# Low-rank A, B and three small pieces of work moved in the opening and the adapter stage of a two-layer kernel

## The chip, the cores and the metric

One of the eight cores of a Trainium2 chip runs the kernel. The time is device microseconds of one launch; the median of 3 runs of the kernel before is 611.19 us (611.18 to 611.63). Everything is float32; TensorE work that is written as float32r is split by hand into a leading part and a rest.

## The reference

`x` is 32 sequences of 64 tokens of 1024 features, with one adapter id (0 to 15) per sequence. Cut to what matters:

```python
c   = einsum('bsi,boi->bso', x, weight[ids])            # a 1024x1024 adapter per sequence
h   = c @ lora_A.T ; logits = c @ W_router.T            # rank 16, 8 experts
w   = normalised top-2 of softmax(logits)
x   = x + c @ W_base.T + b_base + 2 * einsum(h, lora_B, w)
x   = x + ffn(weights1[ids] applied to x)               # 16 heads of 64, hidden 256, exact gelu, features permuted
```

## The kernel before, in words

**Stage 1, the adapters.** The sequences are sorted by id on the chip and worked as 16 pairs, t = 0 to 15. A pair is 8 blocks (k = 0 to 7) of 8 matmuls on TensorE (PE); block k of pair t needs x of the pair (`x_in`, two halves in turn, fetched on ScalarE's DMA queue by `load_x`, L876) and the k-th 128 rows of one or two adapters (`ring`, 512 KB each, on SyncE's (SP's) queue, `load_pair`, L332). The rows of pair t + 1 are asked for when block k of pair t is done (`block_done`), those of pair 1 at once behind the eight of pair 0. Pair 0 has both its sequences on one adapter (`twin_blocks`, L551); the others go through `adapter_blocks` (L535). Between blocks 4 and 5 of pair t, PE does `router(t - 1)` (L571): low-rank A and the router weights, `ar_sb`, 1024 rows of 136 floats (544 bytes) in HBM, against pair t - 1's transposed result `c_pair`. PE waits for `ar_in`, the landing of `ar_sb`, at L622, after pair 0 and ahead of the first block of pair 1.

**VectorE (DVE)** takes each pair's result out by `turn_pair(t)` (L1102, 16 transposes of 32x256 straight from PSUM), then does one more piece of work, then `route(t)` (L1121: a copy at L1135, top-2 and the weights, a chain of 16 small instructions that ends in `hw_four`). In a loop of three rounds (i) over four pairs (n = 0 to 3, t = 4i + 1 + n), that one more piece is a third of a 128x1024 tile of W_base for n < 3 (`turn_tile`, L1182), and for n = 3 `turn_four` (L1197), which transposes four pairs' `hw_four` into `hw_lines` by 16 transposes of 32x128. ScalarE (ACT) then copies `hw_lines` out (`hw_put`, L901). `turn_four` waits for four routes and for the copies of the round before.

**GpSimd (POOL)** moves each `c_pair` into `c_all` (`keep_pair`, L461), then issues gathers by row index: rows of W_base (`raw_tile`) after pairs 0, 4 and 8, and for t in `GATHERS` (L63, pairs 4 to 11) one 128-row piece of low-rank B and of the bias (L479 to L482). B is read by PE at the end of stage 1 (L639), the bias by DVE behind L1242.

**The opening.** SP, ACT and POOL start DMAs at once: ACT the ids and then `ar_sb` (L848), POOL five gathers of W_base of 512 KB (L459), which PE transposes (`turn_base`, L589) and ACT copies back (`base_copied`, L888) before pair 0 starts. ACT's first use of its function table is that copy. DVE sorts in the meantime and releases x and the first adapter by `lists_ok`. `stay_busy` (L596) is eight idle transposes of PE between W_base and pair 0.

**The end of stage 1.** DVE does `turn_pair(14)`, three subtractions (`base_rest`, L1177), two register loads of sequence numbers (`last_seqs`, L249), and `hw_turned`, `route(14)`. Stage 2 (L1245 on) is then 32 steps bound by PE and is not touched.

Of the kernel before, what the change touches and what calls it, by code (L numbers as in the profile page):

```python
# [35 lines left out]
P = 128  # L36
# [6 lines left out]
KT = D // P  # L43
SQ = 32
PAIRS = SEQS // 2
# [14 lines left out]
BUSY = 8  # L60
BATCHED = PAIRS - 4
TILE_PIECES = (range(0, 6), range(6, 11), range(11, 16))
GATHERS = range(PAIRS // 4, PAIRS // 4 + KT)  # L63


def build(nc, xT, x_seq, ids, adapters, w_base, b_base, lora_a_router, lora_b, mix, up, down, perm, out):
# [3 lines left out]
    with ctx:  # L70
        def sem(name):
            return ctx.enter_context(nc.semaphore(name))
# [10 lines left out]
        def at(offset, name, shape, dt=F32):  # L83
# [62 lines left out]
        ar_sb = at(ar_at, "ar_sb", [P, KT, AR])  # L146
# [21 lines left out]
        ident = at(region(0.5), "ident", [P, P])  # L168
# [8 lines left out]
        m1, m2, gap, th, best1, best2, w1, w2 = (  # L177
            (small[5] if i < 4 else small[6])[:, 2 * (i % 4):2 * (i % 4) + 1] for i in range(8))
# [14 lines left out]
        def base_set(j):  # L193
# [11 lines left out]
        ids_in, sort_ids_in, perm_in, ar_in, b_in, bias_in, mix_in, up_in = (  # L205
            sem(n) for n in ("ids_in", "sort_ids_in", "perm_in", "ar_in", "b_in", "bias_in", "mix_in", "up_in"))
# [9 lines left out]
        ident_ok, consts, number_ok, sorting, placed_ok, sorted_done, order_ok = (  # L216
            sem(n) for n in ("ident_ok", "consts", "number_ok", "sorting", "placed_ok", "sorted_done", "order_ok"))
        base_four_ok = sem("base_four_ok")
        loads_ok, lists_ok, tile_in, tile_turned, hw_turned_ok, hw_placed = (
            sem(n) for n in ("loads_ok", "lists_ok", "tile_in", "tile_turned", "hw_turned_ok", "hw_placed"))  # L220
# [5 lines left out]
        router_done, gap_ok, tanh_ok, chain, hw_ok, hw_tr_done, hw_t_ok = (  # L226
            sem(n) for n in ("router_done", "gap_ok", "tanh_ok", "chain", "hw_ok", "hw_tr_done", "hw_t_ok"))
# [21 lines left out]
        def last_seqs(eng):  # L249

            return [eng.value_load(order[0:1, 2, (z + 1) * PAIRS - 1:(z + 1) * PAIRS], min_val=0, max_val=SEQS - 1)
                    for z in range(2)]
# [171 lines left out]
        def _(pool):  # L424
# [47 lines left out]
            for t in range(PAIRS - 1):  # L472
                keep_pair(t)
                if t % 4 == 0 and t // 4 < KT - SOON:
                    j = t // 4 + SOON
                    if t > 0:
                        pool.wait_ge(tile_turned, t // 4)
                    gather(raw_tile[:, :], w_base, perm_sb[:, j:j + 1], tile_in)
                if t in GATHERS:  # L479
                    j = t - GATHERS[0]  # L480
                    gather(b_rows[:, j, :], lora_b, perm_sb[:, j:j + 1], b_in)
                    gather(bias[:, j:j + 1], bias_rows, perm_sb[:, j:j + 1], bias_in)  # L482
            pool.wait_ge(base_hi_ok, 5)
# [361 lines left out]
        def _(act):  # L845
            act.dma_start(all_ids[:, :], ids.rearrange("(a s) -> a s", a=1).broadcast_to([SEQS, SEQS])) \
                .then_inc(sort_ids_in, 16)
            act.dma_start(ar_sb[:, :, :], lora_a_router.rearrange("(k p) e -> p k e", p=P)).then_inc(ar_in, 16)  # L848


            def out_of_acc(t, half):
# [24 lines left out]
            def load_x(t, half):  # L876

                for z in range(2):
                    seq = act.value_load(order[0:1, 2, bass.ds(t + z * PAIRS, 1)], min_val=0, max_val=SEQS - 1)
                    act.dma_start(x_in[:, half, z, :, :],  # L880
                                  x_seq[bass.ds(seq, 1), :, :, :].rearrange("a p k t -> p (a k) t")) \
                        .then_inc(x_in_in[half], 16)
# [25 lines left out]
                            .then_inc(hw_placed, 1)  # L908

            act.sem_inc(hw_placed, 8)  # L910
            act.wait_ge(lists_ok, 1)
            load_x(0, 0)
            for j in range(SOON):
                base_copied(j)
            load_x(1, 1)
            for half in range(2):
                next_x(half, half)
                tanh(half)
# [12 lines left out]
            seqs = last_seqs(act)  # L931
# [101 lines left out]
        def _(dve):  # L1033
# [68 lines left out]
            def turn_pair(t, half):  # L1102

                dve.wait_ge(block_done, (t + 1) * KT)
                dve.wait_ge(c_kept, t * 2 + 2)
                for q in range(P // SQ):
                    for r in range(P // SQ):
                        last = nc.vector.transpose(  # L1108
                            c_pair[r * SQ:(r + 1) * SQ, :, q * SQ:(q + 1) * SQ],
                            wide[half][q * SQ:(q + 1) * SQ, :, :]  # L1110
                            .rearrange("p h (k r f) -> p (h k) r f", k=KT // 2, f=SQ)[:, :, r, :])
                last.then_inc(c_pair_ok, 2)
# [8 lines left out]
            def route(t, hw_out=hw[:, :]):  # L1121

                n = [0]

                def link(ins):

                    n[0] += 1
                    ins.then_inc(chain, 1)  # L1130
                    dve.wait_ge(chain, t * LINKS + n[0])

                logits = h_l[:, ER:AR]
                dve.wait_ge(router_done, t + 1)
                link(nc.vector.tensor_copy(h_l[:, :], router_ps[:, 0:AR]))  # L1135
                link(nc.vector.reduce_max(m1, logits, AX_X))
                link(nc.vector.scalar_tensor_tensor(out=score[:, :], in0=logits, scalar=m1,
                                                    in1=ahead[:, :], op0=ALU.is_equal, op1=ALU.mult))
                link(nc.vector.reduce_max(best1, score[:, :], AX_X))
                link(nc.vector.tensor_scalar(first[:, :], score[:, :], best1, None, ALU.is_equal))  # L1140
                link(nc.vector.scalar_tensor_tensor(out=rest[:, :], in0=first[:, :], scalar=BIG,
                                                    in1=logits, op0=ALU.mult, op1=ALU.add))
                link(nc.vector.reduce_max(m2, rest[:, :], AX_X))
                nc.vector.tensor_tensor(gap, m1, m2, ALU.subtract).then_inc(gap_ok, 1)  # L1144
                link(nc.vector.scalar_tensor_tensor(out=score[:, :], in0=rest[:, :], scalar=m2,
                                                    in1=ahead[:, :], op0=ALU.is_equal, op1=ALU.mult))
                link(nc.vector.reduce_max(best2, score[:, :], AX_X))
                link(nc.vector.tensor_scalar(second[:, :], score[:, :], best2, None, ALU.is_equal))
                dve.wait_ge(tanh_ok, t + 1)
                nc.vector.tensor_scalar(w1, th, 1.0, None, ALU.add)  # L1150
                link(nc.vector.tensor_scalar(w2, th, -1.0, 1.0, ALU.mult, ALU.add))
                link(nc.vector.tensor_scalar(mixw[:, :], first[:, :], w1, None, ALU.mult))
                link(nc.vector.scalar_tensor_tensor(out=mixw[:, :], in0=second[:, :], scalar=w2,
                                                    in1=mixw[:, :], op0=ALU.mult, op1=ALU.add))
                nc.vector.tensor_tensor(hw_out.rearrange("p (e r) -> p e r", r=RANK),
                                        h_l[:, 0:ER].rearrange("p (e r) -> p e r", r=RANK),
                                        mixw[:, :].rearrange("p (e a) -> p e a", a=1).broadcast_to([P, EXPERTS, RANK]),
                                        ALU.mult).then_inc(hw_ok, 1)
                assert n[0] == LINKS
# [34 lines left out]
                if pieces[-1] == 15:  # L1194
                    last.then_inc(tile_turned, 1)

            def turn_four(i):  # L1197


                dve.wait_ge(hw_ok, i * 4 + 4)  # L1200
                dve.wait_ge(hw_placed, i * 8 + 8)
                for q in range(P // SQ):
                    for r in range(P // SQ):
                        last = nc.vector.transpose(hw_lines[q * SQ:(q + 1) * SQ, :, r * SQ:(r + 1) * SQ],
                                                   hw_four[r * SQ:(r + 1) * SQ, :, q * SQ:(q + 1) * SQ])
                last.then_inc(hw_turned_ok, 1)

            def pair(t, half):
                turn_pair(t, half)
                hw_turned(t - 1)  # L1210
                route(t)
# [3 lines left out]
            with dve.Fori(0, KT - SOON) as i:  # L1215
                for n in range(4):
                    t = i * 4 + 1 + n
                    turn_pair(t, (n + 1) % 2)
                    if n < 3:
                        turn_tile(i, TILE_PIECES[n])  # L1220
                    else:
                        turn_four(i)
                    route(t, hw_four[:, (n + 1) % 4, :])
            pair(PAIRS - 3, 1)
            turn_pair(PAIRS - 2, 0)
            for j in SPLIT_ORDER[0:3]:
                base_rest(j)
            seqs = last_seqs(dve)
            hw_turned(PAIRS - 3)
            route(PAIRS - 2)  # L1230
            out_of_acc(PAIRS - 1, 1)
# [164 lines left out]
```

## Time and profile before

| | us |
|---|---|
| median of 3 runs | 611.19 |
| time of the profiled execution | 612.55 |
| span of its profile | 610.7 |
| PE busy, of the span | 593.5 (97%) |
| DVE busy | 471.6 (77%) |
| ACT, POOL busy | 144.7, 128.5 |
| mean DMA traffic | 175 GB/s |

The span is that of the profiled execution, from its first instruction to its last; 1.85 us of that execution's own time lie around it. Times in the rows count from the span's start. Stage 1 ends near 276 us.

### The profile page before, as it was taken

Reading aid. Unit: us, or ns where it says so; the run is one execution under the profiler, and the core shown is the slowest. Engines: PE = TensorE matmul, PEld = TensorE weight load, DVE = VectorE, ACT = ScalarE, POOL = GpSimd, SP = SyncE. Lnnn points to the kernel's source line nnn. Section 1 sums busy time; section 2 is a strip of 40 time slices with the busy share of each in tenths; the row PEclk is TensorE's granted clock in tenths of the full one; section 3 lists DMA queues with packets and bytes.
Section 4 is the critical chain, followed back from the end, with each engine's and each line's share of the span. In section 5 each row is a group of like instructions: output and inputs, shape, how many; then the busy total and the mean of one; then the engine's idle time right before and its main releaser. Section 6 shows DMA issues by size and latency. Waiting matters only on the chain.

```text
span 610.7 us, 13500 instructions
## 1 busy us (share of the span) xinstructions
PE 593.5 (97%) x4383; PEld 349.0 (57%) x4384; DVE 471.6 (77%) x1303; ACT 144.7 (24%) x290; POOL 128.5 (21%) x195
## 2 busy tenths in 40 slices
PE   4999999999998999989999999999999999999997
PEld 3344444344433444457767676767676767676773
DVE  3068778878887779698888897879987889887863
ACT  3100000200020002154333523225342325231324
POOL 4010002121111220060022231313131313131312
PEclk9999999999999999999999999999999999999999
DMA  8998998998999987111022222222232223231322
GB/s 264 407 394 315 309 301 293 325 312 301 315 409 402 355 310 254 44 59 39 17 65 90 74 87 71 87 71 91 63 94 68 88 64 97 62 93 60 94 72 86
DMA packets 43427, 106.90 MB, mean 175 GB/s; under 512 B 8450, under 2 KB 17666, under 8 KB 43394
## 3 DMA queue, kind: packets, MB, share of 16 engines
q1 hardware_dynamic: 30914, 76.04, 36.0%
q0 software_dynamic: 6784, 21.51, 10.6%
q10 hardware_dynamic: 5696, 8.95, 4.3%
q8 instruction: 16, 0.26, 0.2%
q14 instruction: 17, 0.14, 0.1%
HBM read 98.09 MB, written 8.39 MB: 174 GB/s over the span
## 4 chain that ended last, share of the span: by engine, by line
PE 86%; DVE 6%; DMA 4%; issue 1%; DVEq 0%; SPq 0%; ACTq 0%; POOL 0%; another core or an unknown queue 0%
PE wide L546 26%; PE bank L653 20%; PE bank L661 10%; PE bank L741 8%; PE wide L724 8%; PE y_wide L577 4%; DVE c_pair L1108 3%; DMA ring<-adapters_dram 3%; PE y_wide L699 3%; PE wide L561 2%; DMA x_in<-x_seq_dram 1%; PE bank L674 1%; PE bank L677 1%; PE bank L673 1%; PE bank L754 1%
## 5 line engine op out<-in xcount | busy, mean ns | idle before, releaser
L546 PE MATMUL wide<-ring,x_in 128*64 128x512 f32 x960 | 209.5, 592 | 1.8 <-DMA ring<-adapters_dram 1.5
L546 PEld LDWEIGHTS wide<-ring,x_in 128*64 128x64 f32 x960 | 73.0, 137 | 126.7 <-issue 126.7
L1306 DVE STREAM_TRANSPOSE x_tok<-xres 32x128 f32<-32x128 f32 x464 | 140.3, 302 | 6.0
L1108 DVE STREAM_TRANSPOSE c_pair<-wide 32x256 f32<-32x256 f32 x240 | 107.1, 446 | 39.5 <-issue 22.1
L955 ACT ACTIVATE act_sb<-wide 128x512 f32<-128x512 f32 x120 | 66.3, 608 | 191.3 <-PE wide L724 191.3
L653 PE MATMUL bank<-c_hi,base_t 128*128 128x512 f32 x384 | 102.3, 390 | 0.0
L430 POOL DMA_INDIRECT xres<-xT_dram,row_in x32 | 34.3, 1073 | 230.1 <-DVE out_sb L1296 226.8
L653 PEld LDWEIGHTS bank<-c_hi,base_t 128*128 128x128 f32 x384 | 71.9, 188 | 15.4
L661 PE MATMUL bank<-c_lo,base_t 128*128 (+1 forms) x256 | 78.0, 390 | 0.0
L468 POOL COPY c_all<-c_pair 128x512 f32 x30 | 19.4, 672 | 213.7 <-DVE c_pair L1108 213.7
L870 ACT ACTIVATE small<-small 128x1 f32<-128x1 f32 x16 | 3.2, 203 | 218.2 <-DVE small L1144 218.2
L741 PE MATMUL bank<-act_sb,down_sb 64*64 64x512 f32 x224 | 54.3, 602 | 0.0
L741 PE MATMUL wide<-act_sb,down_sb 64*64 64x512 f32 x224 | 54.3, 602 | 0.0
L661 PEld LDWEIGHTS bank<-c_lo,base_t 128*128 128x128 f32 x256 | 48.1, 188 | 10.3
L1287 DVE TENSOR_TENSOR xres<-wide,xres 128x512 f32<-128x512 f32 x28 | 19.4, 692 | 27.1 <-PE wide L741 27.1
L1260 DVE SCALAR_TENSOR_TENSOR xres<-bank,bias,xres 128x512 f32<-128x512 f32 x32 | 23.9, 749 | 19.4 <-PE bank L677 19.4
L653 PE MATMUL bank<-c_hi_slots,base_t 128*128 (+1 forms) x128 | 38.1, 419 | 0.0
L577 PEld LDWEIGHTS y_wide<-ar_sb,c_pair 128*64 128x64 f32 x512 | 30.4, 137 | 9.4 <-issue 6.1
L577 PE MATMUL y_wide<-ar_sb,c_pair 128*64 128x136 f32 x512 | 32.7, 280 | 1.2 <-DVE c_pair L1117 0.8
L495 POOL DMA_INDIRECT out_dram<-out_sb,row_out x28 | 28.5, 1017 | 8.5 <-issue 8.5
L653 PEld LDWEIGHTS bank<-c_hi_slots,base_t 128*128 128x128 f32 x128 | 21.6, 188 | 13.8 <-issue 10.9
L699 PEld LDWEIGHTS y_wide<-mix_now,x_tok 64*64 64x64 f32 x960 | 19.5, 134 | 16.2 <-issue 16.2
(166 smaller groups left out, 605.1 us busy)
## 6 DMA issues: line engine op xcount, KB each, us to landing
ring<-adapters_dram SPq DMA_DIRECT2D x128, 512.0 KB, 5.9
x_in<-x_seq_dram ACTq DMA_DIRECT2D x32, 256.0 KB, 4.9
down_sb<-down_dram SPq DMA_DIRECT2D x32, 128.0 KB
up_raw<-up_dram SPq DMA_DIRECT2D x62, 64.0 KB
ar_sb<-lora_a_router_dram ACTq DMA_DIRECT2D x1, 544.0 KB, 4.3
mix_sb<-mix_dram SPq DMA_DIRECT2D x32, 16.0 KB
xres<-xT_dram,row_in POOLq DMA_INDIRECT x32, 3.4
out_dram<-out_sb,row_out POOLq DMA_INDIRECT x28, 2.9
```

The lines of the kernel that those rows point to most:

```text
L430: pool.indirect_dma_start(dst, None, table, bass.IndirectOffsetOnAxis(ap=rows, axis=0)) \
L495: pool.indirect_dma_start(out_rows, bass.IndirectOffsetOnAxis(ap=row_out[:, j:j + 1], axis=0), src, None).then_inc(stored, 16)
L546: last = pe.matmul(acc[half][h][z * TOK:(z + 1) * TOK, :], x_in[:, half, z, k, :], ring[:, k, z, h * HALF:(h + 1) * HALF], start=(k == 0), ...
L577: last = pe.matmul(router_ps[toks, 0:AR], c_pair[:, k, toks], ar_sb[:, k, :], start=(k == 0), stop=(k == KT - 1), skip_group_check=True)
L653: pe.matmul(c_bank(g, j)[:, :], base_t[:, j, w, k, :], c_hi_row(g, k), start=(k == 0 and w == 0), stop=False)
L661: last = pe.matmul(c_bank(g, j)[:, :], base_t[:, j, 0, k, :], c_lo[:, k, bass.ds(g * GT, GT)], start=False, stop=False)
L699: last = pe.matmul(y_wide[h * HD:(h + 1) * HD, z, p * TOK:(p + 1) * TOK], x1_tok[rows, p * P + h * HD:p * P + (h + 1) * HD], mix_now[rows, ...
L724: last = pe.matmul(u_ps[2 * m + head][:, :], w[rows, m * P:(m + 1) * P], y[rows, :], start=(n == 0), stop=(n == 2))
L741: last = pe.matmul(ps[head * HD:(head + 1) * HD, :], down_sb[rows, j % 2, head, m, :], act_sb[rows, 2 * m + head, :], start=(m == 0), stop ...
L955: nc.scalar.activation(act_of(g, j)[:, i, :], u_ps[i][:, :], ACT.Gelu).then_inc(act_ok, 1)
L1108: last = nc.vector.transpose(c_pair[r * SQ:(r + 1) * SQ, :, q * SQ:(q + 1) * SQ], wide[half][q * SQ:(q + 1) * SQ, :, :] .rearrange("p h (k ...
L1306: last = nc.vector.transpose(x1_tok[q * SQ:(q + 1) * SQ, :].rearrange("p (c f) -> p c f", f=P)[:, :, f * SQ:(f + 1) * SQ], xres[f * SQ:(f ...
```

## The change

It consists of five pieces. The load of `ar_sb` moves from ACT's second instruction to behind `load_x(1, 1)`, the load of x of pair 1; PE's wait at L622 stays. The pieces of B and bias are gathered after pairs 1 to 8 (0-based; the second to the ninth) and no longer after 4 to 11. `turn_four` is cut in two: a quarter of it (4 transposes) goes behind `route` of n = 2, the other three quarters stay at n = 3. ACT makes a one-column copy of `ident` before it waits for the sorted lists, so that its table is loaded there. DVE's `last_seqs` moves ahead of `turn_pair(14)`.

```diff
-GATHERS = range(PAIRS // 4, PAIRS // 4 + KT)
+GATHERS = {j + 1: (j,) for j in range(KT)}
...
-                if t in GATHERS:
-                    j = t - GATHERS[0]
+                for j in GATHERS.get(t, ()):
                     gather(b_rows[:, j, :], lora_b, perm_sb[:, j:j + 1], b_in)
                     gather(bias[:, j:j + 1], bias_rows, perm_sb[:, j:j + 1], bias_in)
...
             act.dma_start(all_ids[:, :], ids.rearrange("(a s) -> a s", a=1).broadcast_to([SEQS, SEQS])) \
                 .then_inc(sort_ids_in, 16)
-            act.dma_start(ar_sb[:, :, :], lora_a_router.rearrange("(k p) e -> p k e", p=P)).then_inc(ar_in, 16)
...
             act.sem_inc(hw_placed, 8)
+            act.wait_ge(ident_ok, 2)
+            nc.scalar.copy(th, ident[:, 0:1])
             act.wait_ge(lists_ok, 1)
             load_x(0, 0)
             for j in range(SOON):
                 base_copied(j)
             load_x(1, 1)
+            act.dma_start(ar_sb[:, :, :], lora_a_router.rearrange("(k p) e -> p k e", p=P)).then_inc(ar_in, 16)
...
-            def turn_four(i):
-                dve.wait_ge(hw_ok, i * 4 + 4)
-                dve.wait_ge(hw_placed, i * 8 + 8)
-                for q in range(P // SQ):
+            def turn_four(i, qs):
+                if qs[0] == 0:
+                    dve.wait_ge(hw_ok, i * 4 + 4)
+                    dve.wait_ge(hw_placed, i * 8 + 8)
+                for q in qs:
...
-                last.then_inc(hw_turned_ok, 1)
+                if qs[-1] == P // SQ - 1:
+                    last.then_inc(hw_turned_ok, 1)
...
                     if n < 3:
                         turn_tile(i, TILE_PIECES[n])
                     else:
-                        turn_four(i)
+                        turn_four(i, range(1, 4))
                     route(t, hw_four[:, (n + 1) % 4, :])
+                    if n == 2:
+                        turn_four(i, range(0, 1))
             pair(PAIRS - 3, 1)
+            seqs = last_seqs(dve)
             turn_pair(PAIRS - 2, 0)
             for j in SPLIT_ORDER[0:3]:
                 base_rest(j)
-            seqs = last_seqs(dve)
```

## Rows read from the trace of the kernel before

**Rows 1.** The page: span, busy us by engine, issue of A (KB, us to landing).

```profile
span 610.7 us, 13500 instructions
...
PE 593.5 (97%) x4383; PEld 349.0 (57%) x4384; DVE 471.6 (77%) x1303; ACT 144.7 (24%) x290; POOL 128.5 (21%) x195
...
ar_sb<-lora_a_router_dram ACTq DMA_DIRECT2D x1, 544.0 KB, 4.3
```

**Rows 2.** Waits of PE, 0 to 300 us: sum in us, times, longest.

```profile
PE wide L546 <- DMA ring<-adapters_dram: 1.5, 2, 1.3
...
PE y_wide L577 <- DVE c_pair L1108: 0.5, 1, 0.5
```

**Rows 3.** Chain of waits, 0 to 45 us: start, us, what.

```profile
10.19 8.06 DMA x_in<-x_seq_dram
...
18.29 13.95 PE wide L561 x64
32.24 8.58 PE wide L546 x40
```

**Rows 4.** Timeline of PE, 7 to 19 us: start, us, what, [idle before <-releaser].

```profile
7.33 1.09 PE L526 MATMUL bank<-ident,base_rows 128*128 128x128 f32 x4 [2.53 <-DMA base_rows<-w_base_dram,perm_sb]
...
12.24 0.60 PE L526 MATMUL bank<-ident,base_rows 128*128 128x128 f32 x4
```

**Rows 5.** Timeline of ACT and its queue, same columns.

```profile
1.16 0.45 ACTq L848 DMA_DIRECT2D ar_sb<-lora_a_router_dram  x1
9.08 1.46 ACTq L880 DMA_DIRECT2D x_in<-x_seq_dram  x2
10.57 1.28 ACT L891 ACT_TABLE_LOAD   x1 [10.44 <-issue]
```

**Rows 6.** DMA queues, 2.2 to 5.2 us: packets, MB, share of 16 engines.

```profile
q10 hardware_dynamic: 1040, 0.56, 68.7%
q0 software_dynamic: 21, 0.09, 22.9%
```

**Rows 7.** DMA queues, 9.7 to 25.3 us.

```profile
q1 hardware_dynamic: 1059, 3.88, 62.0%
```

**Rows 8.** DMA queues, 20.6 to 25.3 us.

```profile
q1 hardware_dynamic: 380, 1.37, 73.7%
q10 hardware_dynamic: 287, 0.52, 29.5%
```

**Rows 9.** DMA queues, 25.3 to 32 us.

```profile
q1 hardware_dynamic: 744, 2.72, 101.6%
```

**Rows 10.** Source view of line 338, 16 to 24 us: durations ns min/median/max.

```profile
L338 SPq DMA_DIRECT2D ring<-adapters_dram x8: 333/340/1415, 16.9 to 22.2; - x8
```

**Rows 11.** Windows at the end: busy us of PE, PEld, DVE, ACT, POOL; granted clock; DMA.

```profile
606.00:608.00 2.00, 0.89 (x10) 0.29 (x5) 0.85 (x2) 0.00 (x0) 1.32 (x2) 1.00 0.18 63
...
609.00:610.00 1.00, 0.00 (x0) 0.00 (x0) 0.00 (x0) 0.00 (x0) 0.00 (x0) 0.72 0.68 262
```

**Rows 12.** Timeline of DVE around pairs 3 to 7, same columns as rows 4.

```profile
94.73 7.34 DVE L1108 STREAM_TRANSPOSE c_pair<-wide 32x256 f32<-32x256 f32 x16 [1.73 <-PE wide L546]
102.11 5.05 DVE L1204 STREAM_TRANSPOSE hw_lines<-hw_four 32x128 f32<-32x128 f32 x16
107.91 0.30 DVE L1135 COPY h_l<-y_wide 128x136 f32<-128x136 f32 x1 [0.76 <-remote]
...
111.82 7.34 DVE L1108 STREAM_TRANSPOSE c_pair<-wide 32x256 f32<-32x256 f32 x16 [0.40 <-issue]
...
157.76 7.34 DVE L1108 STREAM_TRANSPOSE c_pair<-wide 32x256 f32<-32x256 f32 x16 [0.37 <-PE wide L546]
```

**Rows 13.** Timeline of POOL, pair 4.

```profile
106.19 0.95 POOL L430 DMA_INDIRECT bias<-b_base_dram,perm_sb  x1 [0.31 <-issue]
```

**Rows 14.** Timeline of DVE, pair 14.

```profile
254.10 7.34 DVE L1108 STREAM_TRANSPOSE c_pair<-wide 32x256 f32<-32x256 f32 x16 [1.64 <-PE wide L546]
261.47 4.32 DVE L1179 TENSOR_TENSOR base_t<-base_rows,base_t 128x1024 fp32r<-128x1024 f32 x3
```

## The prediction

> **What bounds the kernel now.** The page first: PE is busy 593.5 of 610.7 us [rows 1], so an edit gains only where PE waits, and loses wherever it makes PE wait anew. The waits of PE over stage 1 are few: 1.5 us for adapter rows, once 1.3 us, and 0.5 us for one pair's transposes [rows 2]. The chain of the opening says what starts PE: x of pair 0, 8.06 us under way, lands at 18.25, PE begins pair 0 at 18.29 and pair 1 without a gap at 32.24 [rows 3]. All of this hangs on the DMA engines, so the queues come next. SP's queue alone fills them: from 25.3 to 32 us it takes 101.6% of 16 engines [rows 9].
>
> **A behind x of pair 1.** This is the part that decides. PE's wait for A stays ahead of pair 1, so A must be in by 32 us. What stands behind that wait is the whole adapter stream, then everything else on PE.
>
> What A costs the queue: its 1024 packets of 544 bytes took 68.7% of 16 engines for 3.0 us, over 65 packets an engine 32 ns each [rows 6]. At its old place nothing else wanted the engines: A had moved 0.56 MB by 5.2 us, the gathers of W_base 0.09 [rows 6], and A landed at 1.16 + 4.3 = 5.5 us [rows 1, 5]. The start therefore gains little: at least 0, at most the 2.1 us that A kept the engines. I take 0.2, the nearer row being that the gathers hardly met it. The table load of 1.28 us [rows 5] comes off ACT's first copy of W_base, but x is sent ahead of it, at 9.08, and x is what PE waits for: 0.
>
> At its new place A goes behind x of pair 1 in the same queue, whose packets run from 20.6 to 25.3 us [rows 8], and all the while SP's queue is full. How two queues share is seen there. x is 0.52 MB in packets of 2 KB, 16 an engine; beside it SP's queue moved 1.37 MB, 21 packets of 4 KB an engine. A share by bytes would have let x pass beside 0.52 MB. So the engines take turns by packet, and a small packet waits for a large one each time. A packet of SP's queue is 161 ns (2.72 MB, 664 packets, 41.5 an engine, in 6.7 us) [rows 9]. A is 64 packets an engine, twice 32, so 64 turns of 161 + 32 ns: 12.35 us. With x over at 25.3 - 0.2 = 25.1, A's last packet ends at 37.45, and with the 0.3 us from there to the landing as at the old place it is in at 37.8. Is SP's queue full so long? Of its first 16 loads (8.39 MB, pair 0 and half of pair 1) 3.88 MB are through by 25.3 [rows 7]; 4.51 MB are left, 69 packets an engine, over 64. That gives the upper bound as well: 25.3 + 69 x 0.161 + 64 x 0.032 + 0.3 = 38.8, and 0.7 for a slower engine (x took 4.7 us where 16 turns are 4.0 [rows 8]). Pair 1 starts at 37.8 instead of 32.24: **+5.6**, in the bounds 0 (rival 1) and +7.3.
>
> PE then idles some 5.8 us, and its clock is at stake. After PE's last work at 606.9 us the granted clock is 0.72 of full over 609 to 610 [rows 11], so it fell from 2.4 to 1.2 GHz after about 2.5 idle us. In the opening the first transposes ran 1.09 us for four, the later ones 0.60, from 12.2 us on: 4.7 us after work began [rows 4]. PE would restart at 1.2 GHz and, if it takes as long, lose half of 4.7: **+2.35**, bounds 0 and 2.35; I take the upper one since the idle time is over twice 2.5.
>
> Loads for pair 2 are asked for as pair 1's blocks end and so come later by as much, on engines that are then less full: no further loss, and none of the delay is won back, since PE sets the pace after it.
>
> **`turn_four` in two.** Sixteen transposes take 5.05 us, 0.32 each [rows 12]; four moved are 1.26 us less at pair 4. That is the pair whose lateness PE feels: `turn_pair(5)` began at 111.82, and router(5) waited 0.5 us [rows 2]. The four go behind route(3), where DVE idled 1.73 us before pair 4's transposes [rows 12]. But the gathers of B are now at pair 3 too, and they cost DVE time: at pair 4 the bias gather ended at 107.14 [rows 13], and route's first copy, ready at 107.16, began at 107.91; at pair 7, which had a gather, DVE idled only 0.37 us before the next pair's transposes, against 1.73 at pair 3 without one [rows 12]. So cover falls from 1.73 to 0.37, pair 4's transposes start about 0.9 us late, within 0.1 us of what router(4) allows: +0.05. Net of that DVE is 1.26 - 0.9 = 0.3 us earlier, plus 0.76 if its copy now comes ahead of the bias gather instead of behind it: the wait of 0.46 goes. If the copy falls behind the gather, the gain turns into 0.8 us of loss. I take **-0.4**, bounds -0.5 and +0.8. In the third round nothing is short.
>
> **B in pairs 1 to 8.** It removes 16 packets of gathered rows from pair 9, ahead of the one long wait for adapter rows (1.3 us [rows 2]); 64 KB is 16 packets of 4 KB, one an engine, 0.16 us and as much again at its edge for the bias: **-0.2**, bounds 0 and -0.3. POOL itself has time in every pair.
>
> **Register values ahead of pair 14.** DVE idles 1.64 us before pair 14's transposes, which hides them; where they stood they ran under three subtractions of 4.32 us that DVE's engine was busy with [rows 14]: 0 either way.
>
> The sum: +5.6 + 2.35 - 0.4 - 0.2 = +7.3 us (the 0.2 of the start is in the first term). Against the profiled execution, 612.55 us (span 610.7 and 1.85 around it), that is 619.9; the median is 1.36 us lower, so **618.5 us**. In this forecast's own range stand 615.5 (clock kept, A at 37) to 621.5 (all upper bounds).
>
> **Rivals.**
>
> 1. *A gets through in time.* If a turn takes many small packets, A is quick: 64 packets (2.0 us) behind eight of SP's (1.3 us) end at 28.4, in at 28.7, ahead of 32.04. It decides at 6.6 us over 64 packets, 0.10 us a packet: below it PE does not wait. Then the sum is -0.2 - 0.4 - 0.2: 610.4 us. Against it stand rows 8, where x had at most one packet for each of SP's. The Trainium skill (DMA: Bandwidth & Descriptors, Queues, rings and completion order) has this rule: an engine drains about 9 to 17 descriptors, at most 64, from one ring before it switches. With all 64 in one turn that would be this rival; with 17 for A and SP's loads of 8 an engine it would be four turns and a landing near 32.7. The trace does not decide it for packets of 544 bytes. Chance 0.16.
>
> 2. *A holds up SP's queue.* SP's loads stood up to 1415 ns at issue where 333 are usual [rows 10]: something fills up. If A's 1024 packets keep SP's last three loads back, SP's queue has 45 packets an engine beside A: 25.1 + 45 x 0.193 + 19 x 0.032 + 0.3 = 34.7, +2.5, and with the other terms +1.9: 613.1 us; 615.4 if the clock falls in that wait. Chance 0.13.
>
> 3. *The start was held by A after all.* Then up to 2.1 us come back, and if A is also in time the kernel takes 608.8 us. Against: rows 6. Chance 0.06. With the forecast's stall it would only shift it.
>
> 4. *The halved `turn_four` does not do what it should*, because the copy falls behind the bias gather: 1.2 us more, 619.7, a third of the forecast's chance and inside it.
>
> **How the numbers follow.** The forecast has 0.64, the rest 0.01. A measurement of this kernel can tell 0.2% from no change, 1.22 us: slower means over 612.4. Slower: the forecast and nearly all of rival 2, 0.76; same: rival 1 and a little of 2, 0.18; faster: rival 3, 0.06. The range leaves out rivals 1 and 3: 611.5 to 621.5, rival 2 with A still earlier as its lower end.
>
> **What would show it.** Right: PE waits for the landing of A at pair 1, about 5.8 us from 32; the queue of ACT has 1024 packets from 25 to 37 us beside a full queue of SP; pair 1's first matmuls start at twice their spacing; router(5) without its 0.46 us; pair 10's wait for adapter rows at 1.1 us; the table load near 2 us and x of pair 0 within 0.3 us of 18.2. Wrong: A's packets in one bunch between 25 and 29 us with SP's queue standing still, or a gap in SP's queue after 30 us, or pair 0 that starts a microsecond or more earlier.

## The result and the profile after

The changed kernel takes 621.51 us (median of 4 runs, 619.02 to 623.77) against 611.40 us before (4 runs, 611.18 to 611.63): the ratio is 1.0164, with a 95% interval of 1.0125 to 1.0204. The profiled execution of the changed kernel took 623.77 us, 2.3 us over its median; the profiled execution before took 612.55.

First the page of the changed kernel, the lines that answer to [rows 1]:

```profile
span 622.0 us, 13501 instructions
...
PE 597.7 (96%) x4383; PEld 356.6 (57%) x4384; DVE 471.6 (76%) x1303; ACT 145.2 (23%) x291; POOL 128.5 (21%) x195
...
ar_sb<-lora_a_router_dram ACTq DMA_DIRECT2D x1, 544.0 KB, 19.3
```

The span is 11.3 us longer and PE is only 4.2 us busier, on the same 4383 matmuls. So most of the loss is PE standing still, and a part is matmuls that take longer. A needs 19.3 us from issue to landing where it needed 4.3.

The waits of PE from 0 to 300 us, which answer to [rows 2] (sum in us, times, longest):

```profile
PE wide L545 <- issue: 7.7, 1, 7.7
...
PE wide L525 <- DMA base_rows<-w_base_dram,perm_sb: 3.1, 2, 2.8
...
PE wide L545 <- DMA ring<-adapters_dram: 1.1, 2, 0.6
PE bank L584 <- DVE hw_four L1156: 1.0, 1, 1.0
```

One wait is new, 7.7 us at L545. Router(5)'s 0.5 us is gone, and 1.1 us of waits for adapter rows are left of 1.5. The wait of 1.0 us for `hw_four` of pair 14 is as before. The new wait is put down to "issue", which names nothing. The chain of waits says what is in it (start, us, what; it answers to [rows 3]):

```profile
8.01 9.27 DMA base_rows<-w_base_dram,perm_sb
...
17.32 1.98 PE wide L525 x8
...
21.43 19.30 DMA ar_sb<-lora_a_router_dram
40.73 1.75 issue
42.49 11.50 PE wide L545 x40
53.99 1.85 PE y_wide L576 x32
```

A lands at 40.73, and only then come 1.75 us of something else, before pair 1's first block. The timeline of PE gives the rest (start, us, what, [idle before <-releaser]):

```profile
17.32 1.97 PE L525 MATMUL wide<-ident,base_rows 128*128 128x128 f32 x8 [2.80 <-DMA base_rows<-w_base_dram,perm_sb]
...
20.82 13.95 PE L560 MATMUL wide<-ring,x_in 128*64 128x512 f32 x64
42.49 11.50 PE L545 MATMUL wide<-ring,x_in 128*64 128x512 f32 x40 [7.71 <-issue]
...
198.29 1.94 PE L545 MATMUL wide<-ring,x_in 128*64 128x512 f32 x8 [0.45 <-DMA ring<-adapters_dram]
200.83 10.52 PE L545 MATMUL wide<-ring,x_in 128*64 128x512 f32 x48 [0.60 <-DMA ring<-adapters_dram]
```

From this the 11.3 us of this execution can be added up (40 matmuls at 8.75 us are in the timelines of experiments 1 and 3):

- The opening is 2.53 us longer: pair 0 starts at 20.82 instead of 18.29 [rows 3]. PE waits 2.80 us for the fifth gathered tile of W_base, then transposes it slowly (eight in 1.97 us). Below it turns out that this belongs to this execution, not to the change.
- PE waits for A from the end of pair 0 (20.82 + 13.95 = 34.77) to 40.73: 5.96 us.
- The 1.75 us behind the landing.
- Pair 1's first 40 matmuls take 11.50 us; the same 40 take 8.75 where PE has not stood still: 2.75 us.
- Together 12.99. Back come 0.46 us at router(5), and 0.78 at the adapter rows (0.45 + 0.60 here; before 0.23 + 0.32 + 1.28). The 0.45 us that are left are small gaps not assigned to anything.

The clock stands in the windows (from:to and length in us; busy time and count of PE, PEld, DVE, ACT, POOL; granted clock, share of the DMA engines, GB/s):

```profile
34.80:37.70 2.90, 0.00 (x0) 0.00 (x0) 2.73 (x7) 0.00 (x0) 0.00 (x0) 1.00 1.03 389
37.70:40.70 3.00, 0.00 (x0) 0.00 (x0) 2.92 (x7) 0.00 (x0) 0.00 (x0) 0.50 0.71 258
42.50:48.00 5.50, 5.50 (x14) 1.90 (x16) 0.00 (x0) 0.00 (x0) 2.13 (x3) 0.50 0.41 107
48.00:54.00 6.00, 6.00 (x32) 2.23 (x30) 0.00 (x0) 0.00 (x0) 0.00 (x0) 1.00 0.76 249
```

PE stops at 34.8. Some 3 us later the granted clock drops to 0.50, which is 1.2 GHz. It stays there through the wait and for 5.5 us of work after it: 14 matmuls in 5.5 us, then 32 in 6.0.

Last the DMA queues from 29 to 37 us, which answer to [rows 9] (packets, MB, share of 16 engines):

```profile
q1 hardware_dynamic: 752, 2.73, 86.6%
q10 hardware_dynamic: 750, 0.41, 17.3%
```

SP's queue (q1) moved 752 packets of 4 KB while ACT's queue (q10) moved 750 of 544 bytes: one for one. Over the same 8 us the kernel before moved 825 and 133. A's 1024 packets ran from 27.45 to 40.12 us, 12.7 us; alone they took some 3 [rows 6].

### The profile page after: what moved, and what is told of

It is laid out like the page before. It is cut to its first block, busy times and chain, and to the rows that moved or that the text cites. A ratio compares the mean times of both kernels' runs of the same rounds, so it can differ in the third digit from the quotient of the medians.

```text
span 622.0 us, 13501 instructions
## 1 busy us (share of the span) xinstructions
PE 597.7 (96%) x4383; PEld 356.6 (57%) x4384; DVE 471.6 (76%) x1303; ACT 145.2 (23%) x291; POOL 128.5 (21%) x195
## 4 chain that ended last, share of the span: by engine, by line
PE 87%; DMA 7%; DVE 2%; issue 1%; POOL 1%; ACTq 0%; DVEq 0%; SPq 0%; ACT 0%
PE wide L545 29%; PE bank L652 20%; PE bank L660 9%; PE bank L740 8%; PE wide L723 8%; PE y_wide L576 4%; DMA ar_sb<-lora_a_router_dram 3%; PE y_wide L698 2%; DMA ring<-adapters_dram 2%; DMA base_rows<-w_base_dram,perm_sb 1%; PE bank L672 1%; PE bank L676 1%; PE bank L673 1%; DVE c_pair L1109 1%; PE bank L753 1%
## 5 line engine op out<-in xcount | busy, mean ns | idle before, releaser
L545 PE MATMUL wide<-ring,x_in 128*64 128x512 f32 x960 | 212.2, 598 | 8.8 <-issue 7.7
L545 PEld LDWEIGHTS wide<-ring,x_in 128*64 128x64 f32 x960 | 77.7, 138 | 131.7 <-issue 131.7
L1265 DVE SCALAR_TENSOR_TENSOR xres<-bank,bias,xres 128x512 f32<-128x512 f32 x32 | 23.9, 749 | 19.4 <-PE bank L676 19.4
L576 PE MATMUL y_wide<-ar_sb,c_pair 128*64 128x136 f32 x512 | 32.7, 279 | 0.8 <-DVE c_pair L1118 0.8
## 6 DMA issues: line engine op xcount, KB each, us to landing
ar_sb<-lora_a_router_dram ACTq DMA_DIRECT2D x1, 544.0 KB, 19.3
```

The costliest lines, as they stand in the source:

```text
L545: last = pe.matmul(acc[half][h][z * TOK:(z + 1) * TOK, :], x_in[:, half, z, k, :], ring[:, k, z, h * HALF:(h + 1) * HALF], start=(k == 0), ...
L576: last = pe.matmul(router_ps[toks, 0:AR], c_pair[:, k, toks], ar_sb[:, k, :], start=(k == 0), stop=(k == KT - 1), skip_group_check=True)
```

## The experiments

Eleven runs, on chips that also ran the kernel before. Where a kernel was timed in several rounds, the 95% interval of the ratio stands with it. The expectations of experiments 1 to 4 counted on 1.9 us that the changed kernel seemed to win back between pairs 5 and 10. No time shows them: experiments 1, 3 and 4 came out 1.4, 1.4 and 1.8 us above what was expected, experiment 2 came out 1.7 us below.

**1. A back at the front, the rest of the change kept** (a_front).

```diff
+            act.dma_start(ar_sb[:, :, :], lora_a_router.rearrange("(k p) e -> p k e", p=P)).then_inc(ar_in, 16)
...
             load_x(1, 1)
-            act.dma_start(ar_sb[:, :, :], lora_a_router.rearrange("(k p) e -> p k e", p=P)).then_inc(ar_in, 16)
```

> The changed kernel with the load of low-rank A back at ACT's second instruction; the other four pieces stay. Theory (all of the loss is A's new place): A lands near 5.5 us, no wait ahead of pair 1, pair 0 begins near 18.3 us, and the 1.9 us that the changed kernel won back between pairs 5 and 10 stay: 609.5 us. Rival one (the early table load or something else moved the opening): pair 0 begins near 20.8 us, 611 to 612 us. Rival two (the small pieces gain nothing by themselves, PE only waited less because it came later): 611.2 us.

Measured: 610.86 us (10 runs) against 611.34 (25 runs), ratio 0.9986 (0.9966 to 1.0005). A lands 4.3 us after its issue. The timeline of PE:

```profile
17.77 13.95 PE L560 MATMUL wide<-ring,x_in 128*64 128x512 f32 x64 [1.85 <-DMA x_in<-x_seq_dram]
31.55 8.75 PE L545 MATMUL wide<-ring,x_in 128*64 128x512 f32 x40
```

Pair 1 follows pair 0 without a gap and at full speed. Everything in the change except A's place is worth a gain of at most 0.34% by this interval, or nothing; experiment 9 narrows it.

**2. Only A moved, the rest as before** (a_only): in the kernel before, the same one line moved.

```diff
-            act.dma_start(ar_sb[:, :, :], lora_a_router.rearrange("(k p) e -> p k e", p=P)).then_inc(ar_in, 16)
...
             load_x(1, 1)
+            act.dma_start(ar_sb[:, :, :], lora_a_router.rearrange("(k p) e -> p k e", p=P)).then_inc(ar_in, 16)
```

> The kernel before with nothing but A's load moved behind x of pair 1. Theory: the same wait of some 7.7 us ahead of pair 1, half clock after it, and without the gains at pairs 5 and 10: 1.9 us more than the changed kernel, near 623.4 us. Rival (another piece has a part in the stall): at or under the changed kernel's 621.5 us.

Measured: 621.72 us (4 runs) against 611.34, ratio 1.0158 (1.0123 to 1.0193). The chain:

```profile
19.37 19.42 DMA ar_sb<-lora_a_router_dram
38.79 1.75 issue
40.55 10.86 PE wide L546 x40
```

The one line makes the whole loss, with the same three pieces: pair 0 ends at 18.52 + 13.95 = 32.47 and A lands at 38.79 (6.32 us), 1.75 us follow, and 40 matmuls take 10.86. Here pair 0 began at 18.52, so the late opening of the changed kernel's profile does not come with A. Nor was there a wait at router(5), though B's gathers were late in this kernel and its `turn_four` whole.

**3. PE's wait for A moved behind the blocks that don't read A** (wait_late).

```diff
-            pe.wait_ge(ar_in, 16)
             landed = landings(1)
             adapter_blocks(0, 1, range(0, 3), landed)
             adapter_blocks(0, 1, range(3, 5), landed)
+            pe.wait_ge(ar_in, 16)
             router(0)
```

> The changed kernel with PE's wait for A moved from ahead of pair 1 to ahead of router(0), five blocks later; A's load itself is as late as in the changed kernel. Theory (only the wait's place makes A's slow arrival cost anything): A again takes about 19 us from issue to landing, but router(0) wants it near 43 us, so PE does not wait, the clock stays at full rate; 609.5 us if pair 0 begins at 18.3 us, 612 us if it begins at 20.8 us. Rival (the adapter stream is held up by A's packets): PE waits for adapter rows in pair 1 instead, 613 us or more.

Measured: 610.91 us (10 runs) against 611.34, ratio 0.999 (0.9974 to 1.0005). The view of the tile `ar_sb`, then the timeline of PE:

```profile
L916 ACTq DMA_DIRECT2D ar_sb<-lora_a_router_dram x1: 457/457/457, 19.6 to 19.6; - x1
...
DMA to landing us min/median/max: 19.2/19.2/19.2
```

```profile
32.45 8.75 PE L545 MATMUL wide<-ring,x_in 128*64 128x512 f32 x40
41.03 2.02 PE L576 MATMUL y_wide<-ar_sb,c_pair 128*64 128x136 f32 x32
```

A is as late as in the changed kernel (19.6 + 19.2 = 38.8), and nothing waits for it: pair 1 starts at once, and router(0), the first reader, at 41.03. So the slow load alone costs nothing, and it doesn't hold up adapter rows. What costs is a wait placed 8.6 us ahead of the first reader. The margin is about 2 us.

**4. A in 128 packets of 4352 bytes** (a_wide). The same numbers lie in DRAM in another order, so that each partition reads one run; the wait stays where the change has it.

```diff
-            act.dma_start(ar_sb[:, :, :], lora_a_router.rearrange("(k p) e -> p k e", p=P)).then_inc(ar_in, 16)
+            act.dma_start(ar_sb[:, :, :], lora_a_router.rearrange("p (k e) -> p k e", e=AR)).then_inc(ar_in, 16)
...
+        .reshape(KT, P, AR).transpose(1, 0, 2).reshape(P, KT * AR),
```

> The changed kernel with A laid out in HBM as one contiguous run of 4352 bytes per partition, 128 pieces instead of 1024, at the same late place and with the same wait of PE. Theory (the engines take turns by packet, so the count of packets sets A's time beside a full queue): 8 packets an engine, 8 turns of 161 + 170 ns or 2.7 us; A lands 3 to 4 us behind x of pair 1, near 30 us, no wait at pair 1; 609.5 us (612 us with the late opening). Rival (its place behind x or its bytes make A late): it lands near 40 us as before and the time is 619 to 622 us.

Measured: 611.32 us (10 runs) against 611.34, ratio 0.9995 (0.9979 to 1.001). A lands 10.8 us after its issue at 18.0, ahead of the end of pair 0 at 31.8. The queues from 23.9 to 28 us, in which A passed:

```profile
q1 hardware_dynamic: 296, 1.09, 66.1%
q10 hardware_dynamic: 162, 0.57, 35.4%
```

The same bytes in an eighth of the packets pass in 4 us instead of 12.7. So it is mainly the number of packets, not of bytes, that fixes how long this load takes beside a full queue. The count isn't one for one here: SP's queue moved 296 packets beside 162, of which 128 are A's.

**5. A in 512 packets of 1088 bytes** (a_half), for a second point on that line.

```diff
-            act.dma_start(ar_sb[:, :, :], lora_a_router.rearrange("(k p) e -> p k e", p=P)).then_inc(ar_in, 16)
+            act.dma_start(ar_sb[:, :, :].rearrange("p (k z) e -> p k (z e)", z=2), lora_a_router.rearrange("(k p) e -> p k e", p=P)).then_inc(ar_in, 16)
...
+        .reshape(KT // 2, 2, P, AR).transpose(0, 2, 1, 3).reshape(KT // 2 * P, 2 * AR),
```

> The changed kernel with A in 512 packets of 1088 bytes instead of 1024 of 544. Theory (turns by packet): 32 turns of 161 + 48 ns, 6.7 us where 1024 packets took 12.3 to 12.8 and 128 took some 3; A's time from issue to landing falls from 19.3 to about 13.5 us, PE waits about 2 us and the register loads behind it, mostly at full clock: 612 to 615 us. Rival (packets of less than 2 KB are slow by themselves whatever their count, or the effect is all or nothing): landing as for 544 bytes and 621 us, or as for 4352 bytes and 611.3 us.

Measured: 615.32 us (7 runs, 612.85 to 618.65) against 611.76 (10 runs), ratio 1.0059 (1.0025 to 1.0093). The queues from 26 to 33 us, then the chain:

```profile
q1 hardware_dynamic: 617, 2.24, 80.3%
q10 hardware_dynamic: 520, 0.55, 22.4%
```

```profile
19.83 14.36 DMA ar_sb<-lora_a_router_dram
34.20 1.85 issue
36.05 8.80 PE wide L545 x40
```

A's packets took 7.8 us, from 25.8 to 33.6. With 8, 32 and 64 packets an engine (experiment 4, this one, the changed kernel) they took 4.1, 7.8 and 12.7 us: 0.155 us for each further packet an engine in the first step, 0.153 in the second, on top of some 2.8 us, at the same number of bytes. That is about one packet of SP's queue (0.161 us, worked out in the prediction from [rows 9]) for each of A's. The short end varies, though: in experiment 10 the same 128 packets took 3.1 us, and by that point the first step is 0.19 us a packet.

PE stood still for 2.02 us here, nearly all of it the piece behind the landing, and the clock held: 40 matmuls in 8.80 us. But the wait for A itself was only 0.17 us, since pair 0 began late, at 19.28, and took 14.75 us instead of 13.95: after 3.05 us of idle time in the opening the granted clock was at 0.50 from 17.5 to 20.9. So about half of this execution's loss is its opening and not A. The time came out 0.3 us over the range expected, and the runs lie apart: three took 612.85 to 613.45 us at a mean granted clock of 0.999 to 1.0, three 616.4 to 618.65 at 0.991 to 0.994, which is what the changed kernel's runs have (0.989 to 0.994). That PE lost its clock at the wait for A in these three is likely, but none of them was profiled.

**6. The register loads ahead of the wait** (loads_first). What stands between A's wait and pair 1's first block is `landings(1)` (L531), two loads of a register from SBUF. In the kernel before nothing held PE's sequencer there, so they ran ahead while PE worked.

```diff
-            pe.wait_ge(ar_in, 16)
             landed = landings(1)
+            pe.wait_ge(ar_in, 16)
```

> The changed kernel with PE's four-instruction register load (landings) for pair 1 ahead of the wait for A instead of behind it. In the changed kernel's chain 1.75 us lie between A's landing at 40.73 us and pair 1's first matmul at 42.49. Theory (these are the register loads, which ran under pair 0 as long as A was early): the gap falls below 0.3 us and the time by 1.5 us, to 620.0 us. Rival (the 1.75 us are something that every long wait of PE costs on waking): the gap and the time, 621.5 us, stay.

Measured: 619.71 us (4 runs) against 611.76, ratio 1.0129 (1.0106 to 1.0153), 1.8 us under the changed kernel's median. The chain:

```profile
38.84 0.04 issue
38.89 10.69 PE wide L545 x40
```

The 1.75 us are gone: 0.04 us from landing to first matmul. They were the register loads, which a wait ahead of them had turned from hidden to exposed. The gap shows this; the times alone would not, since one run of the changed kernel took 619.02 us as well.

**7. PE kept busy in the wait** (kept_warm): 64 transposes into a bank that holds nothing then, ahead of the wait. They add work whose result is not used.

```diff
+            for _ in range(64):
+                pe.transpose(bank7[:, 0:P], ident[:, :], ident[:, :])
             pe.wait_ge(ar_in, 16)
```

> The changed kernel with 64 idle transposes of PE (some 7 us at full rate) into an unused bank between pair 0 and the wait for A; the wait ends when it did. Theory (pair 1 lost 2.7 us to the half clock that PE's idling brought): the granted clock stays at full rate, the five blocks ahead of router(0) take 8.7 us instead of 11.5, and the time is 2.1 to 2.7 us less than the changed kernel's 621.5: 619 us. Rival (pair 1's first blocks are slow because the adapter rows or x are late): 621.5 us or more.

Measured: 620.78 us (4 runs, 619.29 to 621.61) against 611.76, ratio 1.0155 (1.0129 to 1.018); the profiled execution took 619.29. The timeline of PE, then the window of pair 1's first blocks:

```profile
31.92 7.21 PE L622 MATMUL bank<-ident 128*128 128x128 f32 x64
40.57 1.94 PE L545 MATMUL wide<-ring,x_in 128*64 128x512 f32 x8 [1.44 <-issue]
```

```profile
40.60:49.20 8.60, 8.60 (x41) 3.47 (x43) 0.00 (x0) 0.00 (x0) 1.24 (x2) 1.00 0.71 243
```

The profile settles it: with PE at work the granted clock stays at 1.00, and the 40 matmuls take 8.80 us in the chain. The mean granted clock of the four runs is 0.997 to 1.0, against 0.989 to 0.994 in the changed kernel. The times don't settle it: the median is 0.7 us under the changed kernel's and not the 2.1 to 2.7 expected, within the spread of four runs of either. A part of the difference is in the profile. A landed at 38.9 (19.08 + 19.8), 6.9 us after pair 0's end at 31.99, the last idle transpose ended at 39.13, and pair 1 began at 40.57. That is 8.58 us from pair to pair where the changed kernel's first profile has 7.71 and its second 6.51, so some of what the clock gave back went into a longer stall. The slow clock is shown as a cost of 1.9 to 2.75 us in the profiles, and not measured as a difference of times.

**8. The kernel before, profiled a second time** (before_again), since two terms of the prediction rested on delays seen once.

> The kernel before, unchanged, for a second profile. Open is whether the two delays in the first one are the kernel's own: route's first copy 1.4 us late at pairs 6, 7, 10 and 11 and 0.8 us late at pairs 4 and 8, and with it router(5)'s wait of 0.46 us. If they come from the gathers of low-rank B they stand at the same pairs again; if they belong to that one execution they are gone or elsewhere, as in the kernel with A alone moved, which kept those gathers and showed none.

Measured: 611.93 us, span 610.1. The timeline of DVE at pair 4, against [rows 12], then the waits of PE from 0 to 300 us:

```profile
102.06 5.05 DVE L1204 STREAM_TRANSPOSE hw_lines<-hw_four 32x128 f32<-32x128 f32 x16
107.15 0.30 DVE L1135 COPY h_l<-y_wide 128x136 f32<-128x136 f32 x1
```

```profile
PE wide L546 <- DMA ring<-adapters_dram: 2.2, 3, 1.0
```

The route copy follows the transposes at once; the 0.76 us ahead of it in the first profile and router(5)'s wait are not there. Both belonged to one execution.

**9. A at the front, timed longer** (a_front_5): the kernel of experiment 1.

> The changed kernel with A's load back at the front once more, over more rounds, for what the other four pieces are worth: the profiles so far show PE waiting 1.2 to 1.6 us for adapter rows after pair 8 with low-rank B gathered early against 1.5 to 2.2 us with it late. Theory (B's gathers took that from the adapter rows): 0.3 to 0.6 us below the kernel before, ratio 0.9990 to 0.9995. Rival (the pieces also free the opening): ratio 0.998 or less. Second rival (nothing): 1.000.

Measured: 611.19 us (11 runs, 610.71 to 612.26) against 611.25 (21 runs), ratio 1.0002 (0.9992 to 1.0011). The rest of the change has no effect within 0.11%.

**10. The wide layout and the late wait together** (both): the edits of experiments 3 and 4, as the version most likely to beat both kernels.

> The changed kernel with A in 128 packets and PE's wait for it ahead of router(0), still behind x of pair 1: the late place without any of its costs. Theory (A's old place did not delay the opening, since the W_base gathers hardly meet it): the same as with A at the front, 610.9 us, and pair 0 begins between 17.7 and 19.3 us as elsewhere. Rival (moving A away frees the opening, hidden so far by the packets of 544 bytes): pair 0 begins near 17 us and the time is 609.5 us.

Measured: 610.93 us (11 runs) against 611.25, ratio 0.9993 (0.998 to 1.0007). A lands 9.9 us after its issue and nothing waits. It repairs the loss, and any gain over the kernel before is at most 0.2%.

**11. The changed kernel, profiled a second time** (after_again).

> The changed kernel unchanged, for a second profile of the opening. In the first one the fifth gather of W_base landed at 17.3 us, PE idled 2.8 us for it, did its transposes at half clock and began pair 0 at 20.8 us; elsewhere it began between 17.8 and 19.3. If the late gather belongs to the one execution, pair 0 begins before 19.5 us here and the time is 1 to 3 us less than that execution's 623.8; if A's absence from the front makes it late each time, it is 20 us or more again. A's 1024 packets again take 12 to 13 us and PE idles 7.5 to 8.2 us.

Measured: 619.2 us, span 617.4. The chain:

```profile
16.95 19.00 DMA ar_sb<-lora_a_router_dram
35.95 1.76 issue
37.71 11.36 PE wide L545 x40
```

Pair 0 began at 17.25 here and at 20.82 in the first profile, and that is most of the 4.6 us between the two executions. A was issued 4.5 us sooner than in the first profile and pair 0 began only 3.6 sooner, so the wait for A was shorter: 35.95 - 17.25 - 13.95 = 4.75 us. PE idled 6.5 us in all, under the 7.5 to 8.2 expected. A's packets ran from 22.9 to 35.3 us, 12.4 us, as expected. What moved the wait is when A was issued: 0.3 us ahead of pair 0's start here, 0.6 behind it in the first profile.

## Why the prediction was right in kind and short in size

The forecast was 618.5 us, in a range to 621.5; the measured median lies at that upper end. Four profiles hold the stall: the changed kernel twice, A alone, and the loads ahead of the wait. Their means say what each term was worth.

- **The wait for A**, forecast +5.6. Measured 5.96, 6.32, 6.43 and 4.75: mean 5.87. The step that led there, turns by single packets, held: 752 against 750 packets in 8 us, and 64 turns took 12.7 us where 12.35 were forecast. Experiments 4 and 5 show it as cause: fewer packets, same bytes, shorter load.
- **The rule of the Trainium skill** (DMA: Bandwidth & Descriptors, Queues, rings and completion order), by which an engine drains some 9 to 17 descriptors of one ring ahead of the next, puts the landing, as estimated in the prediction, near 32.7, some 0.7 us behind the 32.04 at which rival 1 has no wait. Here 752 packets of one queue went beside 750 of the other, and A landed at 38.8 (experiment 2): the trace disagrees, and the measurement decides.
- **The half clock**, forecast +2.35. Measured 2.75, 2.11, 1.94 and 2.61 (40 matmuls against 8.75 us): mean 2.35. That the mean falls on the forecast is in part luck: in the same order the granted clock fell 3.0, 5.4, 3.4 and 4.9 us after PE's last work, not 2.5, and came back 5.5, 4.2, 3.8 and 5.2 us after it began again, where the prediction had 4.7 (its own row gives 12.24 - 7.33 = 4.9). PE idle for 6.4 to 8.1 us brought the clock down each time; idle for 2.02 us (experiment 5) and 2.34 us (the opening of experiment 3) did not, while idle for 2.80 us (the opening of the changed kernel) and 3.05 us (that of experiment 5) was followed by a granted clock of 0.50. Keeping PE at work kept it up (experiment 7).
- **What was missing: +1.75.** This is the step that failed. The prediction says "What stands behind that wait is the whole adapter stream, then everything else on PE"; it did not list the sequencer's own instructions, `landings(1)`, the register loads that the blocks' waits need. Rows of before show them nowhere, since they ran ahead under PE's work. Experiment 6 takes them from behind the wait: the gap falls from 1.75 to 0.04 us, and the median by 1.8.
- **`turn_four` in two**, forecast -0.4. It does what it says, as DVE's timeline of the changed kernel shows:

```profile
106.29 1.24 DVE L1206 STREAM_TRANSPOSE hw_lines<-hw_four 32x128 f32<-32x128 f32 x4
107.89 7.34 DVE L1109 STREAM_TRANSPOSE c_pair<-wide 32x256 f32<-32x256 f32 x16 [0.35 <-PE wide L545]
115.26 3.79 DVE L1206 STREAM_TRANSPOSE hw_lines<-hw_four 32x128 f32<-32x128 f32 x12
119.08 0.30 DVE L1136 COPY h_l<-y_wide 128x136 f32<-128x136 f32 x1
```

  Four of 16 stand a pair earlier, in 1.24 us, and the copy comes 1.26 us sooner after the pair's transposes. But the wait it was to remove was not there in experiment 8, nor in experiment 2 with `turn_four` whole. The term was read from one execution's accident; where that delay is absent its size is 0. The account of B's gathers costing DVE 0.9 us falls with it: with B early (experiments 1 and 4) the copy starts within 0.03 us of the transposes' end. Rival 4 falls as well.
- **B earlier**, forecast -0.2. Waits for adapter rows after pair 8 sum to 1.4 and 1.5 us (A at the front), 1.2 (experiments 3, 4 and 7), 1.6 (experiments 5 and 6), 1.8 (experiment 10) and 1.05 and 1.4 (the changed kernel) with B early; 1.8 and 2.2 before, 1.65 in experiment 2 with B late. That leans to a gain of some 0.4 us, though the two groups overlap. The times of experiments 1, 3, 4, 9 and 10, 0.02 to 0.48 us under the kernel before with intervals that all hold 1, can't confirm it.
- **The opening**, forecast -0.2 within the first term, bound -2.1. Pair 0 began at 18.29 and 18.25 before, and between 17.25 and 20.82 in the changed kernel; with A at the front at 17.77 and 18.33, with A late in experiments 2 to 7 and 10 at 17.86 to 19.28. No place of A orders these. What varies is when the fifth gathered tile of W_base lands (its transposes begin between 13.70 and 17.32) and, behind it, x of pair 0: in 10 of the 13 profiles PE's last wait ahead of pair 0 is for x, 0.2 to 1.9 us. A gain of 2.1 us from the opening (rival 3) is in none of the times, and the spread between executions here, over 3 us, is larger than the term.
- **The table load** was costed at 0 and moved as expected; so were the **register values** ahead of pair 14: PE's wait for that pair's `hw_four` is 1.0 us in both kernels. The timeline of ACT:

```profile
1.24 1.28 ACT L910 ACT_TABLE_LOAD   x1 [1.11 <-PEq L1394]
...
21.43 0.46 ACTq L916 DMA_DIRECT2D ar_sb<-lora_a_router_dram  x1
```

- **Rival 2**, A holding up SP's queue, did not occur: SP's queue kept 86.6% of the engines beside 17.3% of ACT's.

At the median: 5.87 + 1.75 + 2.35 = 9.97 us, against 621.51 - 611.40 = 10.11 measured. The forecast's sum of 7.3 lacked the 1.75, took 0.6 off for two gains that the times do not show, and had the wait 0.3 short. Of the signs named in advance, router(5), the adapter rows (1.1 us), the table load (1.24 to 2.52), the full queue of SP and the slow first matmuls came as written. Pair 0 was not within 0.3 us of 18.2, A's packets ran from 27.5 to 40.1 us instead of 25 to 37, and PE stood still for 7.7 us, not 5.8. Two of the prediction's sums are off by a little, and nothing hangs on them: all upper bounds add up to 621.6 us, not 621.5, and rival 3 to 608.5, not 608.8.

## What to carry to other kernels

A load beside a full queue is priced by its packets: packets per engine times one packet of each queue. Here that is a lower bound: 12.4 to 13.3 us were measured against 12.35 for 64 packets an engine, 7.8 against 6.7 for 32, and 3.1 and 4.1 against 2.7 for 8. Lay small rows out as one run per partition before a load is moved into a busy stretch, and put the wait for it directly ahead of its first reader.

A new wait on an engine costs what is late, and also what its sequencer used to do ahead of time: list register loads and address work behind the wait, and move them ahead of it. Then ask whether PE idles long enough to lose its clock, since that makes the bill longer after the wait is over.

Profile the kernel before twice before a term of half a microsecond is read from one wait.

## What was not expected of the hardware

- Two register loads from SBUF on PE take 1.75 to 1.85 us when they can't run ahead: 40.73 to 42.49 in the chain. They show in no busy time and are put down to "issue".
- After 6 to 8 us of idle time the granted clock stayed at 0.50 for 3.8 to 5.5 us of work (5.5 in the changed kernel's first profile, 42.5 to 48.0), and it fell 3.0 to 5.4 us after PE's last work. Neither is one figure that can be read once and used again.
- The gathers of W_base land up to 3.6 us apart between executions of nearly the same opening, and PE's start with them. In the changed kernel's first profile, after 2.80 us of waiting for the late tile, PE also transposed at half clock (eight in 1.97 us against 1.09); after 2.34 us in experiment 3 it did not.
